# Attention and a top-2 mixture of experts on one core: the load of a block's gates and token numbers moves from sync's queue to gpsimd's

## The reference

```python
x = x + attention(layernorm(x), ctx)            # 8 x 256 tokens of width 256, 16 heads
xf = layernorm(x).reshape(2048, 256)
scores = softmax(xf @ w_gate)                   # 8 experts
weights, idx = top_k(scores, 2)
...                                             # each token goes to 2 experts, at most 1024 tokens per expert
h = einsum('ecd,edf->ecf', exp_x, c_fc);  a, g = split(h, 2)
exp_out = einsum('ecf,efd->ecd', silu(a) * g, c_proj)
out = x + sum over the 2 experts of  gate * exp_out[expert, position]
```

## Time and profile before

| | us |
|---|---|
| median of 3 runs | 533.27 |
| the three runs | 528.49, 534.49, 533.27 |
| time of the profiled execution | 527.09 |
| its span | 525.3 |
| mean granted clock of TensorE, share of full speed | 0.911 |
| PE busy | 433.1 (82%) |
| DVE busy | 252.9 (48%) |
| POOL busy | 177.3 (34%) |
| ACT busy | 175.5 (33%) |

### The profile page before, as it was taken

How to read it: one execution, slowest core, us unless ns; L and a number is a source line. 1 busy time by engine, 2 the same in 40 slices (tenths; PEclk the granted TensorE clock), 3 DMA queues, 4 the chain that set the end, 5 groups by cost and what they waited for, 6 DMA issues and landing times.

```text
span 525.3 us, 8266 instructions
## 1 busy us (share of the span) xinstructions
PE 433.1 (82%) x2218; PEld 255.4 (49%) x2219; DVE 252.9 (48%) x683; ACT 175.5 (33%) x336; POOL 177.3 (34%) x179
## 2 busy tenths in 40 slices
PE   1735794995987979999799887999899999999980
PEld 1512541552643536536345334756566666666650
DVE  4456372583675665756659764442232323222320
ACT  1420452561543635545435453121111221122110
POOL 5631060160280551724431313433233333323322
PEclk9877798996997988969979897999999999999995
DMA  7599469299094290741913162232423332333230
GB/s 236 155 232 211 127 192 271 67 219 274 3 208 146 75 271 12 166 109 62 212 42 112 62 230 82 61 61 41 60 38 52 50 55 40 53 54 48 50 60 3
DMA packets 72693, 59.14 MB, mean 113 GB/s; under 512 B 11976, under 2 KB 69592, under 8 KB 72664
## 3 DMA queue, kind: packets, MB, share of 16 engines
q1 hardware_dynamic: 56072, 41.31, 32.8%
q0 software_dynamic: 7008, 8.43, 9.5%
q10 hardware_dynamic: 9584, 9.05, 5.8%
HBM read 32.89 MB, written 26.46 MB: 113 GB/s over the span
## 4 chain that ended last, share of the span: by engine, by line
DMA 42%; PE 34%; issue 8%; DVE 5%; SPq 4%; POOL 3%; ACTq 2%; ACT 1%; POOLq 1%; DVEq 0%
DMA out<-CTt,GG 28%; PE bank L853 9%; DMA wf<-qparts_d 7%; PE bank L754 5%; DMA wf<-NMT 5%; PE bank L824 4%; PE bank L837 4%; PE bank L733 3%; SPq L385 3%; PE bank L788 2%; PE bank L761 2%; DMA kparts_d<-KP 2%; ACTq L626 2%; POOL slots L504 1%; PE bank L903 1%
## 5 line engine op out<-in xcount | busy, mean ns | idle before, releaser
L1029 DVE TENSOR_REDUCE NEG<-bank 128x2 f32<-128x512 f32 x128 | 85.2, 686 | 79.3 <-PE bank L824 78.4
L903 PE MATMUL bank<-wf,XN 128*128 x304 | 110.2, 499 | 5.0 <-DVE CTt L1252 3.8
L655 ACT ACTIVATE PR<-bank 128x512 f32<-128x512 f32 x128 | 74.8, 595 | 98.9 <-PE bank L837 67.1
L554 POOL DMA_INDIRECT out<-CTt,GG x38 | 58.9, 1551 | 131.5 <-DMA out<-CTt,GG 119.4
L853 PE MATMUL bank<-PR,VA 128*32 128x256 f32 x512 | 86.2, 418 | 0.0
L824 PE MATMUL bank<-KS,wf 99*128 99x256 bf16 x256 | 54.9, 302 | 34.9 <-DMA wf<-qparts_d 26.6
L903 PEld LDWEIGHTS bank<-wf,XN 128*128 128x128 f32 x304 | 54.6, 193 | 41.5 <-issue 16.8
L837 PE MATMUL bank<-wf,KS 102*128 102x256 bf16 x256 | 53.3, 292 | 8.7 <-DMA wf<-NMT 6.4
L696 ACT ACTIVATE XTt<-bank 128x384 f32<-128x384 f32 x38 | 18.7, 491 | 115.6 <-PE bank L916 111.1
L923 PE MATMUL bank<-wp,XTt 128*128 x228 | 55.8, 381 | 0.7 <-ACT XTt L696 0.7
L1245 DVE TENSOR_TENSOR QF<-bank,KF 128x384 f32<-128x384 f32 x38 | 21.2, 557 | 70.8 <-PE bank L903 69.9
(11 more groups left out here) (159 smaller groups left out, 493.1 us busy)
## 6 DMA issues: line engine op xcount, KB each, us to landing
wf<-in_L_ffn_c_fc SPq DMA_DIRECT2D x8, 768.0 KB, 7.5
XG<-slots SPq DMA_DIRECT2D x40, 128.0 KB
slots<-pad_row ACTq DMA_DIRECT2D x7, 645.0 KB, 7.9
slots<-pad_row ACTq DMA_DIRECT2D x8, 516.0 KB, 7.8
kparts_d<-KP SPq DMA_DIRECT2D x8, 384.0 KB, 2.5
qparts_d<-QP SPq DMA_DIRECT2D x8, 384.0 KB
KS<-kparts_d SPq DMA_DIRECT2D x8, 384.0 KB
KS<-kparts_d SPq DMA_DIRECT2D x24, 128.0 KB
```

Source lines behind the costliest of these rows:

```text
L554: pool.indirect_dma_start(out_rows, bass.IndirectOffsetOnAxis(ap=GG[:, u, 1:2].bitcast(U32), axis=0), Y[:, u, :], None, bounds_check=last_ ...
L655: act.activation(PR[:, s % NPROB, :], STB[s % 2][:], ACT.Exp).then_inc(exp_done, 1)
L903: ins = pe.matmul(bank[2 + 2 * u + g][:, 0:FF], XTG[:, u, k, :], wf[:, bass.ds(off + (k * 2 + g) * FF, FF)], start=k == 0, stop=k == KC - 1)
L1029: dve.tensor_reduce(NEG[:, n % 2, t, 2 * hp:2 * hp + 2], MXB[m % 2][:].rearrange("p (i s) -> p i s", i=2), AX.X, ALU.max, negate=True).the ...
```

## The change

`load_gates` leaves SP's list and goes to POOL's, with the same read of the table and the same DMA. The wait on `added` in front of it goes, since POOL has waited for the same store in `add_block` just before. On POOL the load for block t+1 stands right behind the store of block t. The loads of blocks 0 and 1 stand behind the scatter of batch 6 and wait for the first table and the scatters of six batches; the load of block 8 waits for the full table and for all scatters. The loop loads one block more than there is, and POOL waits for that load, and for SP's last loads of rows, at the end. SP keeps only the loads of rows.

```diff
@@ sync @@
-            def load_gates(t, u):
-
-                if later(t, 2):
-                    sp.wait_ge(added, (t - 1) * 16)
-                row = sp.value_load(table[0:1, 0, bass.ds(t, 1)], min_val=0, max_val=XROWS - P)
-                sp.dma_start(GG[:, u, :], slots[bass.ds(row, P), D:RW]).then_inc(gg_in[u], 16)
-
...
             load_block(0, 0)
             load_block(1, 1)
-            load_gates(0, 0)
-            load_gates(1, 1)
...
             for t in range(2, AHEAD):
                 load_block(t, t % 2)
-                if t >= 4:
-                    load_gates(t - 2, t % 2)
...
             for t in range(PEELED, PEELED + 2):
                 load_block(t, t % 2)
-                load_gates(t - 2, t % 2)
             with sp.Fori(0, pairs - PEELED // 2) as i:
                 for u in range(2):
                     load_block(2 * i + PEELED + 2 + u, u)
-                    load_gates(2 * i + PEELED + u, u)
@@ gpsimd @@
+            def load_gates(t, u):
+
+                row = pool.value_load(table[0:1, 0, bass.ds(t, 1)], min_val=0, max_val=XROWS - P)
+                pool.dma_start(GG[:, u, :], slots[bass.ds(row, P), D:RW]).then_inc(gg_in[u], 16)
+
             def add_block(t, u):
                 pool.wait_ge(ys_ready, t + 1)
...
+            pool.wait_ge(ahead_ready, 1)
+            for i in range(2):
+                pool.wait_ge(scattered[i], 16 * TB * TOPK * (KNOWN // 2))
+            load_gates(0, 0)
+            load_gates(1, 1)
             pool.wait_ge(out_stored[0], 16 * KNOWN)
             add_block(0, 0)
             scatter(B - 1)
             for t in range(1, PEELED):
                 add_block(t, t % 2)
+                if t + 1 == AHEAD:
+                    pool.wait_ge(table_ready, 1)
+                    for i in range(2):
+                        pool.wait_ge(scattered[i], 16 * TB * TOPK * (B // 2))
+                load_gates(t + 1, (t + 1) % 2)
             pool.wait_ge(out_stored[1], 16 * (B - KNOWN))
-            pool.wait_ge(table_ready, 1)
             pairs = pool.value_load(npairs[0:1, 0:1], min_val=8, max_val=MAXPAIR)
             with pool.Fori(0, pairs - PEELED // 2) as i:
                 for u in range(2):
                     add_block(2 * i + PEELED + u, u)
+                    load_gates(2 * i + PEELED + 1 + u, 1 - u)
+            pool.wait_ge(gg_in[0], pairs * 16 + 16)
+            for u in range(2):
+                pool.wait_ge(xg_in[u], pairs * 16 + 16)
             pool.wait_ge(added, pairs * 32)
```

## The result

| | us |
|---|---|
| changed kernel, median of 4 runs | 562.29 (561.01 to 563.06) |
| before, median of 4 runs | 530.88 (521.29 to 534.49) |
| ratio, 95% interval | 1.071 (1.058 to 1.084) |
| profiled execution: time, span | 561.8, 560.2 |

The change costs 7.1%. The prediction had 559, in a range of 540 to 588.

A forecast was written before the change was run, and what follows sets the result against it. The landing of one store before the next, not PE, was taken to set 4.87 us a block. (5.6 - 4.87) x 36 = 26.3 plus 0.3 gave +27 on the 533.3 median, 560; forecast 559, range 540 to 588.

The forecast's parts named there:

- the ring of store, load and weighing: Expert blocks: each store, next GG load on POOL, weighing and next store follow one another, 5.6 us a block for 4.87.
- Start: GG load on POOL: starts 1.85 us after the store's start, once POOL's engine is free plus 0.30 us.
- Descriptors: GG load on POOL: writing descriptors takes 0.97 us, like the scatter's, ending 2.8 us after the store's start.
- the rival of the quick descriptors: GG load on POOL: descriptors written at SP's 0.33 us, landing at 3.9 us, kernel loses 14 us, 547; chance 0.15.
- Landing: GG load on POOL: lands 4.2 us after the store's start, between 3.9 and 4.6, behind the store's packets; from above 5.1.
- End of the weighing to the store: DVE to POOL: the next store starts 0.8 us after weighing ends, taken from a row showing 0.88.
- The cover of before: Kernel before: weighing ended 0.85 us ahead of the previous store's landing in one block, some 1.5 where the store takes 3.83.
- The two lengths of a landing: Kernel before: stores land after 3.83 us, every second one 4.4 to 4.5, as SP's XG load shares the engines.
- SP's freedom: SP's XG loads no longer wait behind a store: worth nothing by itself, as PE needs 4.42 us and stores grant 4.87.
- The rival that ended faster: POOL's load skips the engine, starting at 1.1 us and landing at 2.7: 10 us less, 523; chance 0.05.
- the slow stretch of the attention: Attention: PE clock at 0.74 with 83% busy, idle in one piece; cited for a falling clock adding 23 us, 582.
- The end: After the last store: the load for a nonexistent block lands about 0.3 us later, adding 0.3 us.

The follow-up runs named there:

- The control: Kernel before with a GG column pair per block and DVE's copy of token numbers, SP still waiting for the store: 528.07 us, ratio 0.999.
- the two versions that load further ahead: Changed kernel with POOL loading gates two blocks ahead, ratio 0.990; kernel before with SP loading gates without waiting for the store, ratio 0.976.
- the version with the load on SP: Kernel before with a GG column pair per block, SP's gate load waiting for DVE's copy of token numbers instead of the store: 516.92 us, ratio 0.976.

## Why the prediction was right

The mechanism was right: the ring of store, load and weighing closed, the chain changed from the store's landing to GG's, PE's busy share fell from 96% to 81% (about 80% forecast), the clock did not fall, and freeing SP gave nothing in this kernel. The control and the two versions that load further ahead show that the place of the load, and not the load, is the cause. The size came out close, 5.6 us a block forecast and 5.81 measured, partly by luck, since terms were off in opposite ways. The time was closer than the step, which was forecast at 27 us and is 34.9 between the two profiled executions: the 533.3 that it was added to lies 5 us above the 527.8 and 527.9 that the kernel before took in the two later sessions.

| step, from the start S of a store | forecast | block of 443.44 |
|---|---|---|
| the load starts on POOL | S+1.85 | S+1.09 |
| its descriptors end | S+2.8 | S+2.22 |
| it lands | S+4.2 | S+4.39 |
| the weighing ends | S+4.8 | S+4.99 |
| the next store starts | S+5.6 | S+5.94 |

- **Start.** I let the load wait for the engine and the 0.30 us that lie between scatters. Its record starts 0.76 us sooner and overlaps the store's. Of its 1.13 us 0.50 lie beside the store's record and 0.63 behind it, about the 0.59 that a load takes where no store is ahead.
- **Descriptors.** I took the scatter's 0.97 us as the nearest row. A load of 128 pieces of 8 bytes costs 0.6, nearer to SP's 0.33: this is the rival of the quick descriptors, right about that row and wrong about the time.
- **Landing.** This is the term that was mis-sized: I gave it 1.4 us behind the descriptors, by the packets of the store and an own latency as short as the store's first packet. It was 2.17, of which 1.54 is there with nothing ahead. The bound from above, 2.3, was nearly the truth. My reason, the store's packets ahead, covers about half of the 0.6 us that the store adds.
- **End of the weighing to the store.** 0.95 us (0.91 to 0.95 in the loop), where I had shortened the row's 0.88 to 0.8 without a reason. The row should have stood.
- **The cover of before.** In this block the weighing starts at S+4.51 (447.95 - 443.44) for S+1.80, 2.71 us later. With the weighing at S+1.80 this ring alone would have let a store follow after 1.80 + 0.48 + 0.95 = 3.23 us, while stores came every 4.87: the slack was 1.64 us, and the 1.07 left of the 2.71 is what this block's 5.94 has over 4.87. My cover of 0.85 to 1.5 us left out every second block, whose store lands after 4.4 to 4.5 us and where it is 2.1 to 2.2. The 2.71 is made up of 1.05 for the load's place in POOL's list, 0.54 of the store's descriptors, 0.5 for POOL's queue against SP's (2.13 for the 1.64 from 444.47 to 446.11) and 0.6 for the place behind the store.
- **The two lengths of a landing.** The conclusion held, that rows issued 1.25 us behind a store cost it some 0.6 us, but I read the strips wrongly. Queue 0 has POOL's packets, queue 1 SP's (number, MB, share). From 444.43 to 448.43, then from 439.16 to 441.85, and from 453.55 to 456.35:

```profile
q0 software_dynamic: 144, 0.03, 8.4%
...
q1 hardware_dynamic: 211, 0.07, 20.3%
...
q0 software_dynamic: 66, 0.07, 26.8%
q1 hardware_dynamic: 144, 0.00, 2.7%
```

  The store of 444.43 carries only 0.03 MB, because most of that block's slots are empty, and lands after 3.13 us for that reason; the undisturbed landing to compare with is 3.83. In the second stretch queue 0 has no packet at all. Up to 2.69 us behind its start the store of 439.16 has moved nothing, while the rows are half through: they go ahead of it, where I had the store's packets begin at 2.0. In the third, where the rows were issued some 1.6 us behind the store, it is the other way round, and that store lands after 3.83.
- **SP's freedom.** I wrote that it is "worth nothing by itself", since PE needs 4.42 us a block and the stores grant it 4.87. That step failed, though nothing of the sum hung on it: alone it is worth 11 us, because the rows then stay clear of the stores and the stores themselves come faster.
- **The rival that ended faster** had the start right, S+1.09 for its S+1.1, and failed at the rest: the load did use POOL's engine, and needed over 3 us to land and not 1.6. Its other half, the 10 us for stores clear of the rows, was right and is what the version with the load on SP earns: 11 us.
- **Two slips without weight.** The rival of the quick descriptors adds 3.9 + 0.1 + 0.48 + 0.8 to 5.25; it is 5.28, and 15 us instead of 14. And the slow stretch of the attention has its idle time not in one piece but in three waits of PE, of 1.28, 1.04 and 0.73 us between 190 and 195 us; in the changed kernel, with a wait of some 1.2 us in each block, the granted clock stayed at 1.00.
- **The end.** I gave 0.3 us for the load of a block that doesn't exist. From the last store to the end of the span it is 11.7 us (560.2 - 548.5) for 8.9 before. Of these 2.8 us, 0.9 are the wait for that load, which lands at 552.1, 0.9 behind the last store. Most of the rest is POOL's DRAIN at the end of its list; in the changed kernel and in the one before:

```profile
L140 POOLq DRAIN  x1: 7549/7549/7549, 552.4 to 552.4; - x1
```

```profile
L140 POOLq DRAIN  x1: 5793/5793/5793, 519.3 to 519.3; - x1
```

  It takes 7.5 to 7.6 us in each version with one plain load from POOL in a block and 5.8 in each without, but also 5.75 with two loads in a block, so what lengthens it stays open.

## What to carry to other kernels

Before moving a small load from one queue to another, ask what releases its issue and what its landing releases: between a store that it must follow in program order and the operation that the next store waits for, its whole latency enters the pace, less the slack that was there, however few its bytes. The cover of such a load is read as the time from its consumer's end to the event that really comes last, and compared with the whole latency on the new queue, place behind other packets included. And if a queue is to be freed from a wait, give the waiting transfer another buffer rather than another engine: here that gained 2.4%, where the move lost 7.1%.

## What the runs showed of the hardware that was not expected

- POOL's record of a DMA can start while the record of the DMA before it still runs: such a load behind a store takes mostly 1.05 to 1.2 us, and 0.56 to 0.66 alone.
- A load of 1 KB needs 2.1 us to land when POOL issues it and 1.6 when SP does, with nothing ahead of it; behind a store of 128 KB in POOL's queue it takes 3.3.
- SP's loads of rows lengthen a store's landing from 3.8 to 4.4 us when issued 1.25 us behind it and not when issued 1.58 us behind: in the first case the rows' packets go ahead of the store's, in the second behind.
- The 13 us over which the runs of before scatter lie at least in part ahead of the expert blocks. Over the ten profiled executions, whose attention is the same, the first store of a block starts anywhere between 330.2 and 339.9 us. What moves it, no run shows.
